# Local attention with biases of full height, paired row loads, two banks for the first values and earlier exponentials, and a reordered last tile of the experts

## The chip, the cores and the metric

The kernel runs on one core of a Trainium2 chip. The metric is the device time of one launch in microseconds (us), the median of several runs. The engines are named as the profile names them: PE is TensorE (PEld its weight loads), ACT is ScalarE, DVE is VectorE, POOL is GpSimd, SP is SyncE, which here only issues DMAs. Each engine works through its own list in order; semaphores tie the lists together.

## What is computed

The input is 8 sequences of 512 rows of 256 values. Four layers follow one another, each added to the rows it gets: causal attention, a feed-forward layer with attention and four experts, a local attention, and the same feed-forward layer again.

```python
x = x + attn_a(layernorm(x), ...)
x = x + ffn(layernorm(x), ...)       # attention, then the expert that a router picks for each row
x = x + attn_b(layernorm(x), ...)    # the local attention
x = x + ffn(layernorm(x), ...)
```

The change touches the third layer and the end of both expert stages. In the third layer the roles of the axes are swapped: at each of the 512 positions the 8 sequences attend to one another, with 16 heads of 16 values and a table of relative keys.

```python
qkv = einsum('tbe,fe->tbf', query, in_proj_weight) + in_proj_bias
scores = einsum('btd,bsd->bts', q, k) + einsum('btd,tsd->bts', q, rel_k)
attn = einsum('bts,bsd->btd', softmax(scores), v)
out = attn @ out_w.T + out_b
```

The experts compute `relu(x @ W1[e] + b1[e]) @ W2[e] + b2[e]` for the expert `e` of each row, and a second layernorm.

## The kernel before

**Stages.** The program runs the causal attention and the first feed-forward attention interleaved, then the first expert stage (`experts`, k = 0), then `local_attention`, then the second feed-forward attention, and the second expert stage (k = 1). Between stages there is a barrier of all engines.

**Local attention.** The positions are cut into four blocks `bt` of 128 (one per partition). A block holds 8 tiles `t`, one for each sequence, of 128 x 256 values. The steps of a block are:

- ACT normalises the tiles (`norm`, L2299) with a mean and a deviation that DVE (`stats`, L2398, L2402, and `shift_of`, L2407) and POOL (`inv_std`, L2550, L2552, a power of -0.5) have made. For block 0 this goes in two groups of four tiles, `x_half` and `x_loaded`, each with its own DMA; the other three blocks form one group of 24 tiles (`x_rest`).
- PE transposes the tiles (`transpose_x`, L2167) four at a time, and ACT copies the result out (`read_xT`, L2307).
- PE projects each tile: `project_qk` (a bias matmul, L2177, then two float32 matmuls, L2179, into one of the two banks `a_ps`), and `project_v` (L2190, the bias matmul L2191, and L2193 for the relative keys, into the single bank `b_ps`). ACT reads the banks (`read_qk`, L2321 and L2319, and `read_v`, L2326). A float32 matmul appears as two records in the trace.
- POOL makes six of the eight products of queries and keys (`scores`, L2570) and DVE two; DVE sums all eight (L2434) and, once the first four tiles have their sums and all eight values have been read, forms the maximum and subtracts it (`shift`, L2445 to L2449).
- ACT takes the exponentials of half a block (`exp`, L2338 and L2342), POOL multiplies five tiles of values by them (`values`, L2579, L2583) and DVE three, PE sums over keys (L2222), and DVE divides (`normalise`, L2488).
- PE transposes the result (L2234), multiplies it by the output weights (`project_out`, a bias matmul L2242 before each pair of L2244), and DVE adds the rows (`add_residual`, L2494).

The biases are kept exact as the sum of three bfloat16 rows, `bias3` and `bo3`, which are multiplied by three rows of ones, `ones3`. So every bias matmul contracts over 3 partitions, where all others around it contract over 128.

**What sets the order.** Everything is written out by hand, and the code is the order. While block `bt` passes through POOL and DVE, PE and ACT prepare block `bt + 1`: PE's list for a block is the transposes and the eight projections of the next block, with `transpose_att` and `project_out` of the block before it in between, and then the sums of this block. ACT's list holds the reads of the next block, with `exp(bt, 0)` behind `read_projections(bt + 1, 3)` and `exp(bt, 1)` behind `read_projections(bt + 1, 5)`.

POOL writes its products to a ring of four buffers (`ring`); a buffer is free again when DVE or PE has summed it.

**The experts' end.** An expert stage has 35 tiles (`SLOTS`). For each tile `s` DVE adds bias and row and takes the statistics (`add_x1`, L1823 to L1829), POOL makes the deviation (`inv_std`, L1973, L1977), DVE scales (`finish`, L1835, L1841), and POOL stores the rows with an indirect DMA (`store`, L1982). POOL also gathers the rows to be added (`gather_prev`, L1961) and adds a bias to them (`shift_prev`, L1968). The last lines of POOL's list before are:

```python
    shift_prev(s)              # for s in range(SLOTS)
    if s >= 1:
        inv_std(s - 1)
    if s >= 2:
        store(s - 2)
    if s + 1 < SLOTS:
        gather_prev(s + 1)
...
inv_std(SLOTS - 1)
store(SLOTS - 2)
store(SLOTS - 1)
```

## Time and profile before

| | us |
|---|---|
| median of three runs | 2563.73 |
| the three runs | 2557.81, 2563.81, 2563.73 |
| the profiled execution | 2558.12 |
| its span, first to last instruction | 2556.3 |
| PE busy | 2378.2 (93% of the span) |
| DVE busy | 1843.5 (72%) |
| ACT busy | 1404.6 (55%) |
| POOL busy | 1366.8 (53%) |

The span lies 1.8 us below the time of its own execution, and that execution 5.6 us below the median. The local attention lies between 1418.5 us, where SP issues the load of its first rows, and 1710.9 us, where PE begins the next stage. All positions in the text are us from the start of the span. The shares of busy time are means over the whole span and don't tell which engine holds up a stage; that is read from the timeline of the stage.

### The profile page before, as it was taken

The numbers are of one execution on the slowest core, as the hardware profiler recorded it, in microseconds if no ns is written. First come the engines' busy times: TensorE is split into PE (matmuls) and PEld (weight loads), VectorE is DVE, ScalarE is ACT, GpSimd is POOL, SyncE is SP. The second block draws the span as 40 slices with busy tenths as digits, with TensorE's granted clock in tenths as the row PEclk, the third lists the DMA queues.
The fourth block names the chain that finished last, engine by engine and source line by source line (L and its number), as shares of the span: only waits on it lengthen the run. The fifth ranks groups of instructions, "written<-read, shape, count | busy, mean of one in ns | idle before, by whom it ended". The sixth has DMA issues, their size and how long they took to land. (4 is left out here: it accounts for less than half of the span.)

```text
span 2556.3 us, 45358 instructions
## 1 busy us (share of the span) xinstructions
PE 2378.2 (93%) x14436; PEld 1387.8 (54%) x14436; DVE 1843.5 (72%) x3687; ACT 1404.6 (55%) x2991; POOL 1366.8 (53%) x1416
## 2 busy tenths in 40 slices
PE   5999999999999999989999699978999999989998
PEld 3555555554443444349898366653344444349997
DVE  5999999999778888845333567867778888844333
ACT  3666666665777777753333232214777777653332
POOL 6466666653335555444655579843335555445655
PEclk9999999999999999999999799988999999999999
DMA  5333333433334444334654200015434444244654
GB/s 156 108 110 103 113 103 102 121 108 93 118 110 135 128 136 125 90 120 163 214 197 160 71 1 17 17 63 136 118 110 133 131 133 124 79 137 164 205 193 140
DMA packets 253390, 305.85 MB, mean 120 GB/s; under 512 B 32642, under 2 KB 228321, under 8 KB 253156
## 3 DMA queue, kind: packets, MB, share of 16 engines
q1 hardware_dynamic: 241620, 275.37, 35.8%
q0 software_dynamic: 10176, 26.27, 3.1%
q8 instruction: 120, 1.97, 0.3%
q10 hardware_dynamic: 1360, 1.31, 0.2%
q14 instruction: 114, 0.93, 0.1%
HBM read 210.32 MB, written 92.84 MB: 119 GB/s over the span
## 5 line engine op out<-in xcount | busy, mean ns | idle before, releaser
L705 ACT ACTIVATE prob_af<-sct_af 128x512 f32<-128x512 f32 (+1 forms) x864 | 483.6, 582 | 257.7 <-PE sct_af L513 251.2
L784 DVE TENSOR_REDUCE neg_max_af<-sc_af 128x1 f32<-128x512 f32 (+3 forms) x864 | 548.8, 663 | 90.7 <-PE sc_af L490 84.9
L784 DVE TENSOR_REDUCE neg_max_f<-sc_f 128x1 f32<-128x512 f32 x512 | 333.7, 685 | 78.2 <-PE sc_f L490 74.0
L705 ACT ACTIVATE prob_f<-sct_f 128x512 f32<-128x512 f32 x512 | 289.8, 598 | 135.5 <-PE sct_f L513 132.9
L513 PE MATMUL sct_af<-stack_q_af,stack_k_af 99*128 99x512 bf16 (+3 forms) x1024 | 321.7, 345 | 4.5 <-ACT prob_af L705 3.1
L490 PE MATMUL sc_af<-stack_k_af,stack_q_af 96*128 96x512 bf16 (+3 forms) x1024 | 321.5, 344 | 4.2 <-DVE neg_max_af L784 4.2
L1636 PE MATMUL y_ps_e<-w_r,hT_e 128*128 x1120 | 256.3, 382 | 8.8 <-issue 5.2
L541 PE MATMUL out_af<-prob_af,v_aug_af 128*32 128x512 f32 (+3 forms) x2048 | 233.1, 527 | 15.4 <-DVE prob_af L814 14.2
L814 DVE SCALAR_TENSOR_TENSOR prob_af<-prob_af,w_r 128x512 f32<-128x512 f32 (+2 forms) x224 | 229.4, 1032 | 17.4 <-ACT prob_af L705 16.0
L1823 DVE TENSOR_TENSOR y_e<-y_ps_e,b_e 128x256 f32<-128x256 f32 x70 | 29.7, 425 | 290.9 <-PE y_ps_e L1636 281.2
L1636 PEld LDWEIGHTS y_ps_e<-w_r,hT_e 128*128 128x128 f32 x1120 | 207.2, 190 | 40.6 <-issue 14.9
L1649 PEld LDWEIGHTS hT_ps_e<-xT_e,w_r 128*128 128x128 f32 x1856 | 217.2, 193 | 5.5 <-issue 1.5
L1649 PE MATMUL hT_ps_e<-xT_e,w_r 128*128 128x128 f32 x1856 | 218.9, 277 | 1.3 <-ACT xT_e L1708 1.1
L490 PE MATMUL sc_f<-stack_k_f,stack_q_f 96*128 96x512 bf16 x512 | 196.1, 388 | 13.9 <-DVE neg_max_f L784 7.6
L513 PEld LDWEIGHTS sct_af<-stack_q_af,stack_k_af 99*128 99x128 bf16 x1024 | 97.8, 98 | 198.3 <-ACT prob_af L705 114.4
L1708 ACT ACTIVATE xT_e<-xT_ps_e 128x256 f32<-128x256 f32 x70 | 26.9, 384 | 323.7 <-PE xT_ps_e L1627 312.3
L513 PE MATMUL sct_f<-stack_q_f,stack_k_f 99*128 99x512 bf16 x512 | 195.8, 385 | 5.2 <-ACT prob_f L705 4.0
L1719 ACT ACTIVATE hT_e<-hT_ps_e,b_r 128x128 f32<-128x128 f32 x560 | 152.8, 383 | 32.0 <-issue 24.8
L1077 POOL TENSOR_TENSOR parts_af<-qkf_af,parts_af 128x512 bf16<-128x512 f32 x62 | 80.9, 1304 | 132.6 <-ACT parts_af L683 132.4
L490 PEld LDWEIGHTS sc_af<-stack_k_af,stack_q_af 96*128 96x128 bf16 x1024 | 99.3, 100 | 75.7 <-issue 19.6
L541 PE MATMUL out_f<-prob_f,v_aug_f 128*32 128x512 f32 x1024 | 137.0, 607 | 1.0 <-ACT prob_f L705 0.7
L513 PEld LDWEIGHTS sct_f<-stack_q_f,stack_k_f 99*128 99x128 bf16 x512 | 49.7, 98 | 159.4 <-ACT prob_f L705 118.2
(385 smaller groups left out, 4623.0 us busy)
## 6 DMA issues: line engine op xcount, KB each, us to landing
w_r<-in_f_W_dram SPq DMA_DIRECT2D x66, 1024.0 KB, 5.6
...
```

What stands on the lines that cost most here:

```text
L490: last = nc.tensor.matmul(bank[:, o:o + cols], M.stack_q[0:96, g, h, qt * P:qt * P + P], M.stack_k[0:96, g, h, 0:cols], start=not masked, ...
L513: last = nc.tensor.matmul(bank[:, o:o + T - q0], M.stack_k[0:99, g, h, kt * P:kt * P + P], M.stack_q[0:99, g, h, q0:T], start=not masked, ...
L541: last = nc.tensor.matmul(bank[32 * i:32 * i + 32, q0:T], M.v_aug[:, kt, 4 * g + i, :], M.prob[:, kt % 2, i, 0:T - q0], start=(kt == 0), s ...
L705: nc.scalar.activation(dst, src.rearrange("p (h q) -> p h q", h=len(heads)), ACT.Exp).then_inc(S.exp_done, 1)
L784: nc.vector.tensor_reduce(M.neg_max[:, qt, heads[0]:heads[-1] + 1], src, AX.X, ALU.max, negate=True).then_inc(S.max_done, 1)
L814: nc.vector.scalar_tensor_tensor(out=p, in0=p, scalar=1.0, in1=M.floor[:, g % 2, hs, kt * P:T], op0=ALU.min, op1=ALU.max).then_inc(S.clip_ ...
L1077: nc.gpsimd.tensor_tensor(M.parts[:, j, 1, :], full, top, ALU.subtract).then_inc(S.split_step, 1)
L1636: last = nc.tensor.matmul(y_ps[:, 0:D], hT[s % 2][:, c, :], w2[:, c, e, :], start=(c == 0), stop=(c == FC - 1))
L1649: last = nc.tensor.matmul(hT_ps[2 * (s % 2) + f][:, q * P:q * P + P], w1[n % NW][:, c, cols], xT[:, c, :], start=(c == 0), stop=(c == DC - 1))
L1708: nc.scalar.activation(xT[:, :, :], xT_ps[:, 0:D].rearrange("p (c t) -> p c t", c=DC), ACT.Copy).then_inc(xT_ready, 1)
L1719: last = nc.scalar.activation(hT[s % 2][:, 4 * f + q, :], hT_ps[2 * (s % 2) + f][:, q * P:q * P + P], ACT.Relu, bias=b1[:, e, 4 * f + q:4 ...
L1823: nc.vector.tensor_tensor(y[i][:, :], y_ps[:, 0:D], b2[:, e, :], ALU.add).then_inc(y_ready, 1)
```

## The change

**Biases of full height.** `bias3`, `bo3` and `ones3` get 128 partitions in place of 3. POOL fills the new rows of the biases with zeros during tile 9 of the first expert stage (two more memsets, and the one of `ones3` is taller). The three rows of the biases are loaded as before. The number of matmuls and their columns stay.

**Rows in pairs.** The first four tiles of block 0 are loaded by two DMAs of two tiles (`x_first`, `x_half`), and go through `stats`, `inv_std`, `shift_of`, the normalisation and PE's transposes in two pairs. There is one more group of statistics on DVE and on POOL. PE projects queries and keys of tiles 0 to 3 before it transposes tiles 4 to 7.

**First values from two banks.** In block 0 the values of odd tiles go to `att_ps`, those of even tiles to `b_ps`, so that PE waits for the read of the bank two tiles back. ACT normalises block 1 in pairs of tiles between these reads, no longer before them.

**Exponentials sooner.** `exp(0, 0)` stands behind `read_projections(1, 1)`, and `exp(bt, 0)` of blocks 1 and 2 stands ahead of `read_projections(bt + 1, 3)`.

**Last tile of the experts.** POOL takes `inv_std` of tile 33 ahead of the gather of tile 34, stores tile 32 before the deviation of tile 34, and adds the bias to the gathered rows of tile 34 behind that deviation. DVE finishes tile 33 ahead of `add_x1(34)`.

```diff
             for s in range(SLOTS):
+                if s == SLOTS - 1:
+                    finish(s - 1)
                 add_x1(s)
...
-                if s >= 1:
+                if 1 <= s < SLOTS - 1:
                     finish(s - 1)
...
-            for s in range(SLOTS):
+            for s in range(SLOTS - 1):
                 shift_prev(s)
                 if s >= 1:
                     inv_std(s - 1)
                 if s >= 2:
                     store(s - 2)
-                if s + 1 < SLOTS:
-                    gather_prev(s + 1)
+                if s == SLOTS - 2:
+                    inv_std(s)
+                gather_prev(s + 1)
...
+                    pool.memset(L.bias3[:, :], 0.0)
+                    pool.memset(L.bo3[:, :], 0.0)
...
+            store(SLOTS - 3)
             inv_std(SLOTS - 1)
+            shift_prev(SLOTS - 1)
             store(SLOTS - 2)
             store(SLOTS - 1)
...
-    L.bias3, L.bo3, L.ones3 = sb("bias3", [3, NB_COLS], BF16), sb("bo3", [3, D], BF16), sb("ones3", [3, P], BF16)
+    L.bias3, L.bo3, L.ones3 = sb("bias3", [P, NB_COLS], BF16), sb("bo3", [P, D], BF16), sb("ones3", [P, P], BF16)
...
+    def v_bank(bt, t):
+
+        return att_ps if bt == 0 and t % 2 == 1 else b_ps
...
-            sp.dma_start(x[0][:, 0:4, :], x_in[0][:, 0:4, :]).then_inc(x_half, 16)
+            sp.dma_start(x[0][:, 0:2, :], x_in[0][:, 0:2, :]).then_inc(x_first, 16)
+            sp.dma_start(x[0][:, 2:4, :], x_in[0][:, 2:4, :]).then_inc(x_half, 16)
...
+            def transpose_first():
+
+                for u in range(2):
+                    pe.wait_ge(xn_ready, u + 1)
+                    for c in range(DC):
+                        for t in (2 * u, 2 * u + 1):
+                            last = nc.tensor.transpose(g_ps[c][:, t * P:t * P + P], xn[:, t, c * P:c * P + P], C.ident[:, :])
+                        if u == 1:
+                            last.then_inc(tr_made, 1)
...
-                if n >= 1:
+                bank = v_bank(bt, t)
+                if bt == 0 and t >= 2:
+                    pe.wait_ge(b_read, n - 1)
+                elif bt >= 1:
                     pe.wait_ge(b_read, n)
...
-            transpose_x(0, 0)
-            transpose_x(0, 1)
+            transpose_first()
             pe.wait_ge(L.params, NPARAM)
             pe.wait_ge(L.rel_ready, 1)
             pe.wait_ge(L.bias_placed, 16 * 6)
-            for t in range(NTM):
+            for t in range(4):
+                project_qk(0, t)
+            transpose_x(0, 1)
+            for t in range(4, NTM):
                 project_qk(0, t)
...
-            norm(0, range(4))
-            norm(0, range(4, NTM))
+            norm_first(1, x_first, range(2))
+            norm_first(2, x_half, range(2, 4))
             read_xT(0, 0)
+            norm_first(3, x_loaded, range(4, NTM))
+            for t in range(4):
+                read_qk(0, t)
             read_xT(0, 1)
-            for t in range(NTM):
+            for t in range(4, NTM):
                 read_qk(0, t)
-            norm(1)
+            may_norm(1)
             for t in range(NTM):
                 read_v(0, t)
+                if t < 4:
+                    last = norm_tiles(1, (2 * t, 2 * t + 1))
+                    if t == 3:
+                        last.then_inc(xn_ready, 1)
...
                     read_projections(bt + 1, 1)
+                    if bt == 0:
+                        exp(bt, 0)
                     read_xT(bt + 1, 1)
                     read_projections(bt + 1, 2)
                     if bt >= 1:
                         read_oT(bt - 1, 1)
+                        exp(bt, 0)
                     read_projections(bt + 1, 3)
-                    exp(bt, 0)
```

The first place is ACT's list in block 0, from the transposes of block 1 (`xnT_l`) to the first exponentials (`weight_l`, with the small `s_ps_l` for DVE's own tile). `qk_l` and `vr_l` are the reads of `read_qk` and `read_v`. Before:

```order
1611 L2307 ACTIVATE xnT_l<-g_ps_l 128x512 x2
1612 L2321 ACTIVATE qk_l<-a_ps_l 128x512
1613 L2326 ACTIVATE vr_l<-b_ps_l 128x384
1614 L2321 ACTIVATE qk_l<-a_ps_l 128x512
1615 L2326 ACTIVATE vr_l<-b_ps_l 128x384
1616 L2307 ACTIVATE xnT_l<-g_ps_l 128x512 x2
1617 L2321 ACTIVATE qk_l<-a_ps_l 128x512
1618 L2326 ACTIVATE vr_l<-b_ps_l 128x384
1619 L2321 ACTIVATE qk_l<-a_ps_l 128x512
1620 L2326 ACTIVATE vr_l<-b_ps_l 128x384
1621 L2338 ACTIVATE weight_l<-s_ps_l 128x512
1622 L2342 ACTIVATE s_ps_l<-s_ps_l 128x128
```

And now:

```order
1624 L2339 ACTIVATE xnT_l<-g_ps_l 128x512 x2
1625 L2353 ACTIVATE qk_l<-a_ps_l 128x512
1626 L2358 ACTIVATE vr_l<-b_ps_l 128x384
1627 L2353 ACTIVATE qk_l<-a_ps_l 128x512
1628 L2358 ACTIVATE vr_l<-b_ps_l 128x384
1629 L2370 ACTIVATE weight_l<-s_ps_l 128x512
1630 L2374 ACTIVATE s_ps_l<-s_ps_l 128x128
1631 L2339 ACTIVATE xnT_l<-g_ps_l 128x512 x2
```

The exponentials have moved ahead of two copies of transposes and four reads of projections.

The second place is the head of the local attention on ACT: `w_next` is where the normalised tiles go. Before:

```order
1605 L2299 ACTIVATE w_next<-x_l,shift_x_l,rstd_l 128x256 x8
1606 L2307 ACTIVATE xnT_l<-g_ps_l 128x512 x4
1607 L2321 ACTIVATE qk_l<-a_ps_l 128x512 x6
1608 L2319 ACTIVATE qk_l<-a_ps_l 128x256 x2
1609 L2299 ACTIVATE w_next<-x_l,shift_x_l,rstd_l 128x256 x8
1610 L2326 ACTIVATE vr_l<-b_ps_l 128x384 x8
```

And now:

```order
1605 L2317 ACTIVATE w_next<-x_l,shift_x_l,rstd_l 128x256 x4
1606 L2339 ACTIVATE xnT_l<-g_ps_l 128x512 x2
1607 L2317 ACTIVATE w_next<-x_l,shift_x_l,rstd_l 128x256 x4
1608 L2353 ACTIVATE qk_l<-a_ps_l 128x512 x4
1609 L2339 ACTIVATE xnT_l<-g_ps_l 128x512 x2
1610 L2353 ACTIVATE qk_l<-a_ps_l 128x512 x2
1611 L2351 ACTIVATE qk_l<-a_ps_l 128x256 x2
1612 L2358 ACTIVATE vr_l<-b_ps_l 128x384
1613 L2317 ACTIVATE w_next<-x_l,shift_x_l,rstd_l 128x256 x2
1614 L2358 ACTIVATE vr_l<-att_ps_l 128x384
1615 L2317 ACTIVATE w_next<-x_l,shift_x_l,rstd_l 128x256 x2
```

The second four tiles are normalised behind the first copies, and block 1 is normalised by twos between reads that alternate between two banks.

The third place is POOL's list at the end of the first expert stage: `var_e` and `rstd_e` are `inv_std`, L1961 (now L1963) is the gather, L1968 (now L1970) the addition of the bias, L1982 (now L1984) a store. Before:

```order
776 L1961 DMA x_prev_e<-layer_d,xt_r 128x256
777 L1968 TENSOR_TENSOR x_prev_e<-x_prev_e,be_e 128x256
778 L1973 TENSOR_SCALAR var_e<-mv_e 128x1
779 L1977 TENSOR_TENSOR rstd_e<-var_e,minus_half 128x1
780 L1982 DMA layer_d<-out_e,xt_r 4096x256
781 L1973 TENSOR_SCALAR var_e<-mv_e 128x1
782 L1977 TENSOR_TENSOR rstd_e<-var_e,minus_half 128x1
783 L1982 DMA layer_d<-out_e,xt_r 4096x256 x2
```

And now:

```order
778 L1975 TENSOR_SCALAR var_e<-mv_e 128x1
779 L1979 TENSOR_TENSOR rstd_e<-var_e,minus_half 128x1
780 L1963 DMA x_prev_e<-layer_d,xt_r 128x256
781 L1984 DMA layer_d<-out_e,xt_r 4096x256
782 L1975 TENSOR_SCALAR var_e<-mv_e 128x1
783 L1979 TENSOR_TENSOR rstd_e<-var_e,minus_half 128x1
784 L1970 TENSOR_TENSOR x_prev_e<-x_prev_e,be_e 128x256
785 L1984 DMA layer_d<-out_e,xt_r 4096x256 x2
```

The deviation of tile 33 has moved ahead of the last gather, and the addition to the gathered rows behind the deviation of tile 34.

## Rows read from the trace of the kernel before

**Rows 1.** Windows: start:end, length, busy PE, PEld, DVE, ACT, POOL (instructions), PE clock, DMA.

```profile
1428.00:1440.00 12.00, 11.43 (x29) 5.66 (x30) 7.23 (x23) 5.17 (x10) 0.00 (x0) 0.64 0.37 117
1525.20:1586.20 61.00, 60.66 (x258) 40.31 (x257) 48.11 (x33) 18.16 (x36) 56.74 (x16) 1.00 0.05 18
1586.20:1647.10 60.90, 60.56 (x258) 40.22 (x256) 48.47 (x34) 14.23 (x28) 52.36 (x15) 1.00 0.05 18
```

**Rows 2.** Timeline, experts' end: start, duration, engine, line, operation [idle before, releaser].

```profile
1408.89 0.42 DVE L1823 TENSOR_TENSOR y_e<-y_ps_e,b_e 128x256 f32<-128x256 f32 x1 [2.04 <-PE y_ps_e L1636]
1409.93 0.71 POOL L1968 TENSOR_TENSOR x_prev_e<-x_prev_e,be_e 128x256 f32<-128x256 f32 x1 [1.18 <-DMA x_prev_e<-layer_d,xt_r]
1410.62 0.23 POOL L1973 TENSOR_SCALAR var_e<-mv_e 128x1 f32<-128x1 f32 x1
...
1411.70 1.31 POOL L1982 DMA_INDIRECT layer_d<-out_e,xt_r  x1 [0.20 <-issue]
...
1415.84 0.98 POOL L1982 DMA_INDIRECT layer_d<-out_e,xt_r  x1 [0.42 <-issue]
1418.51 0.38 SPq L2136 DMA_DIRECT2D x_l<-layer_d  x1
```

**Rows 3.** Timeline, head of the local attention, all engines.

```profile
1422.18 1.40 DVE L2398 BATCH_NORM_STATS2 st_l<-x_l 128x6 f32<-128x256 f32 x4 [7.12 <-DMA x_l<-layer_d]
...
1425.78 4.04 ACT L2299 ACTIVATE w_next<-x_l,shift_x_l,rstd_l 128x256 f32<-128x256 f32 x8 [23.75 <-DVE shift_x_l L2407]
...
1427.91 1.97 PE L2167 MATMUL g_ps_l<-ident,w_next 128*128 128x128 f32 x8 [19.17 <-ACT w_next L2299]
...
1432.32 0.60 PE L2177 MATMUL a_ps_l<-bias_l,ones_l 3*128 3x512 bf16 x1
...
1442.89 4.19 POOL L2552 TENSOR_TENSOR rstd_l<-var_l,half_l 128x24 f32<-128x24 f32 x1
```

**Rows 4.** Timeline of PE: the projection of one tile, bias to bias.

```profile
1493.59 0.39 PE L2177 MATMUL a_ps_l<-bias_l,ones_l 3*128 3x512 bf16 x1
...
1495.72 1.03 PE L2190 MATMUL b_ps_l<-w_l,xnT_l 128*128 128x256 f32 x4
...
1496.68 0.22 PE L2191 MATMUL b_ps_l<-bias_l,ones_l 3*128 3x128 bf16 x1
...
1497.48 0.39 PE L2177 MATMUL a_ps_l<-bias_l,ones_l 3*128 3x512 bf16 x1
```

**Rows 5.** Timeline of PE in the first stage: tall bfloat16 matmuls around a float32 group.

```profile
307.42 0.38 PE L524 MATMUL sct_af<-stack_q_af,w_r 99*128 99x512 bf16 x1
307.64 1.03 PE L442 MATMUL gen_af<-wa_o,attT_af 128*128 128x256 f32 x4
308.50 0.38 PE L509 MATMUL sct_af<-mask_kq,ident_bf 128*128 128x512 bf16 x1
```

**Rows 6.** Timeline of block 0, from POOL's scores to PE's sums.

```profile
1452.75 26.94 POOL L2570 TENSOR_TENSOR ring_l<-qk_l 128x2048 f32<-128x2048 f32 x6 [5.66 <-ACT qk_l L2319]
...
1475.56 0.49 ACT L2326 ACTIVATE vr_l<-b_ps_l 128x384 f32<-128x384 f32 x1 [2.02 <-PE b_ps_l L2193]
...
1477.62 0.70 DVE L2449 TENSOR_TENSOR s_ps_l<-s_ps_l,peak_l 128x512 f32<-128x512 f32 x1
...
1494.08 0.59 ACT L2338 ACTIVATE weight_l<-s_ps_l 128x512 f32<-128x512 f32 x1
...
1494.84 3.69 POOL L2579 TENSOR_TENSOR ring_l<-vr_l,weight_l 128x2048 f32<-128x2048 f32 x1 [15.15 <-ACT weight_l L2338]
...
1509.06 3.62 PE L2222 MATMUL att_ps_l<-ring_l,ident 128*128 128x256 f32 x16
```

**Rows 7.** Timeline of block 3: POOL's values, two bias matmuls of the last project_out.

```profile
1665.75 18.26 POOL L2579 TENSOR_TENSOR ring_l<-vr_l,weight_l 128x2048 f32<-128x2048 f32 x5 [0.96 <-ACT weight_l L2338]
...
1702.31 0.28 PE L2242 MATMUL g_ps_l<-bo_l,ones_l 3*128 3x256 bf16 x1 [0.69 <-ACT attT_l L2349]
...
1703.58 0.28 PE L2242 MATMUL g_ps_l<-bo_l,ones_l 3*128 3x256 bf16 x1
```

58 lines of the change are left out of this document (32 added, 26 removed).

## The prediction

> **What bounds the kernel now.** The page gives PE 93% of the span, but that is a mean; the change lies in the local attention and at the ends of the expert stages, so I read those. First the windows of PE there: from the end of block 0's sums (1525.2) to that of block 1's is 61.0 us and to that of block 2's 60.9 us more, and in both PE is busy 60.6 of them, at full clock, POOL 52.4 in the second, DVE 48.5 [rows 1]. So blocks 1 and 2 are PE's. Then the timeline of block 0: POOL makes its six score products from 1452.75 to 1479.69 and then sits idle 15.15 us until ACT's exponentials; DVE had the shifted scores ready at 1478.32, ACT took them at 1494.08 [rows 6]. There the order of ACT's list is the bound. Then the head: rows asked for at 1418.51, in at 1422.18, first projection at 1432.32, with PE at half clock (2.4 GHz is 1.00) [rows 2, 3]. Last the experts' end: the deviation of tile 33 (1410.62) stands behind the gather for tile 34 [rows 2].
>
> **The experts' end, twice.** Before, POOL waits for the gather until 1409.93, adds, takes tile 33's deviation at 1410.62, stores three times, the last at 1415.84 [rows 2]. Now the deviation of tile 33 comes before the gather, about 2.7 us earlier, and the last stores follow the deviation of tile 34. DVE can take y of tile 34 only at 1408.89 [rows 2] and needs 1.6 us for its statistics; `finish(33)` now stands before it and may hold it 0.3 us for a store to land. From 1410.8: deviation 0.9, addition 0.7, two stores of 1.3 and 1.0 with 0.6 between: the last starts at 1414.4 in place of 1415.84, **1.5 us** less (bounds 0, if the landing holds DVE longer, and 2.7, the whole advance). The second expert stage has the same rows, so again 1.5 at the end of the program. The two memsets fall in tile 9; POOL waits for gathers in such tiles (1.18 us even at the last [rows 2]), so 0; uncovered, less than 2 us, since a POOL product of 2048 columns takes 3.65 [rows 7] and they have 1264.
>
> **The head.** The load starts at 1417.0. Two tiles in place of four: before, 3.67 us from issue to DVE's start [rows 2, 3]; I take 3.0 (bounds 2.2 and 3.67). Statistics of two tiles 0.9, POOL's deviation at most 1.3, shift 0.2, two tiles on ACT 1.0: the first pair is normalised at about 1423.4, the second at 1424.5, since each step of the second waits for the same step of the first. Four transposes (1.97 for eight at half clock [rows 3]) and two copies later, at 1426.5, PE projects, against 1432.32 [rows 3]. The new order has a bubble of its own: transposes of tiles 4 to 7 and both copies stand between projection 3 and 4 with nothing beside them, 2.0 us. The clock: a mean of 0.64 over 1428 to 1440 [rows 1] means half speed to about 1436.6, 8.7 us after PE began. PE begins 4.3 us earlier, so I let the clock rise by 1432.3: two projections of 3.84 at half clock (half of the second at full), the others 1.93, the bubble, and the last read: 1447.4. A floor is POOL's deviation of 24 tiles, over at 1447.08 before [rows 3] and at 1445.6 now. POOL's scores start at **1447.4** against 1452.75, 5.3 sooner (bounds 1446.0 and 1449.3, the latter with the next projection slow too).
>
> **Biases of full height.** Sixteen float32 records of 256 columns last 3.62 together, 0.38 alone [rows 6], so one takes (3.62 - 0.38) / 15 = 0.216, one of 512 columns 0.432, one of 128 0.108. A projection takes 3.89 from bias to bias, of which 4 x (0.432 + 0.216 + 0.108) = 3.02 is float32 work [rows 4]; the two short biases cost the other 0.87. In the first stage a bfloat16 matmul of 99 or 128 partitions and 512 columns costs 0.22 before a float32 group, and the group (0.86 for 4 x 0.216) loses nothing to the one behind it [rows 5]. By these rows the biases should cost 0.22 and 0.06: a projection 3.30, **0.59 less**. A bias of 256 columns goes from 1.27 - 0.86 = 0.41 [rows 7] to 0.11, 0.30 less. Bounds: 0 and these values; I take these, since the rows are of the same engine, types and widths.
>
> The Trainium skill (TensorEngine Tiling (Array Packing), Key Properties) says that a change of the tiling mode drains the engine; a contraction over 3 rows could be such a mode, and that would be the 0.3 us.
>
> **Block 0.** Eight values are read with two normalised tiles between the first four reads: 1.53 us each on ACT, later 1.3 on PE, so the last is read at about 1459.3 against 1476.05 [rows 6]. DVE's shift waits now for POOL's fourth product (1447.4 + 18.05) and ends at 1469.9. Then ACT, which has reached the exponentials at 1468.0, takes them at once: done at 1470.6. POOL is not through with its scores before 1474.4, so the **15.15 us wait goes whole**, and what is late next is POOL itself. Its values take 18.2 + 7.3 = 25.5: over at 1499.9 in place of 1520.38. PE sums tiles 0 and 1 from 1488.0, waits 1.2 for the third product (1492.6) and ends at 1504.8 against 1525.2: **20.4 us**, which is 5.3 + 15.15. ACT held at the exponentials for 1.9 us delays two copies, which PE first needs for projection 4, 3.3 us after; no cost.
>
> **Blocks 1 and 2.** PE's cycle holds eight projections and eight output biases: 8 x 0.59 + 8 x 0.30 = 7.1 less, 53.8 us. POOL's is 52.4 and DVE's work 48.5 [rows 1], so both now press. Walking the lists, POOL never waits long; DVE's first `normalise` comes 2.0 us late behind its own products, which delays nothing in the next projections but carries into block 3. I take 0.5 us for small waits: cycles of 54.3, **6.6 us less each**, 13.2. In block 3 DVE's chain sets POOL's start, 2.1 us later by the carried delay. So POOL's last values start 20.4 + 13.2 - 2.1 = 31.5 us sooner, at 1634.2 in place of 1665.75 [rows 7]. `exp(1, 0)` and `exp(2, 0)` follow DVE's shift within 0.3 us in this walk, ahead of POOL's need.
>
> **The tail.** After the last sums, eight output biases lie in a row on the path: 8 x 0.30 = **2.4 us**.
>
> **The sum.** 31.5 (with the first 1.5 of the experts) + 2.4 + 1.5 = **35.4 us** from the profiled execution's 2558.12: 2522.7. The median of before lies 5.6 above that execution, two of three runs being near 2563.8 and one at 2557.8. Carried over, 2528.3; I give 2528.
>
> **Rivals.**
>
> *The cycles don't follow PE.* With PE at 53.8, POOL at 52.4 and DVE waiting on both, the lists may interlock: PE's sums need POOL's last product, DVE's own products come behind `normalise`, PE's next projections need those. For it: only 1.4 us of room, and a DVE list that is near 50 before any wait. Against it: DVE had 12.5 us of idle time per cycle [rows 1]. At 57.5 us a cycle 6.4 us are lost: 2528.3 + 6.4 = 2535.
>
> *A bias costs the same at any height.* Then only order counts. The head loses 2.5 us (eight projections), block 0's sums become PE's (eight projections of 3.89 from about 1463) and end at 1511.5, 13.7 sooner; the cycles and the tail stay; 15.2 with the end of the program: 2548.5. For it: the tall matmuls of the first stage stand next to other work than these. Against it: nothing is lost there at a change of type or width, so the height is what is left [rows 5].
>
> The Trainium skill (TensorE: Matmul & The Clock Gate, Why this matters for your kernels) says that one matmul of a short contraction takes the same time as one of 128 rows. By that the change of height gives nothing, and the time would be the one of this rival; the trace speaks against it as far as rows 4 and 5 can be compared.
>
> *The clock falls.* PE, quicker now, waits for POOL and DVE, and after waits it runs at half speed. The row for it: after 19.17 us of idle time PE needed 8.7 us to get back, in which it lost 4.3 us [rows 1, 3]. One such spell per block costs 4 x 4.3 = 17 us and gives 2545; from eight or nine spells on, two per block, the gain of 35.4 is used up, and at ten the program is slower, 2571. It decides if PE's waits in the cycles grow to several us; I count 1.2 us in block 0 and less after, where before they are 0.3 us of 61.
>
> **How the numbers follow.** Forecast 0.66, with a range of 2518 to 2536: from all of it and runs at the lower level (2522.7 - 4) to a bias that saves half of what rows 5 say on PE's cycles, head and tail (+7.5). Interlocked cycles 0.19 (2535, to 2541). Same cost at any height 0.09 (2548). The clock 0.06: half of that near one spell or two per block, 2545 to 2563, half beyond. The 80% range takes in the forecast and the interlocked cycles, and a start of the scores at its late bound: 2517 to 2541. A measurement of this kernel can tell some 0.3% (7.7 us) from no change. Faster by more than that: 0.66 + 0.19 + 0.09 = 0.94; within it 0.03; slower 0.03.
>
> **What would show each step.** Right, if bias matmuls of 512 columns are followed after 0.22 us and a projection takes 3.3 us; if POOL's first values start without a wait near 1474; if the windows between ends of sums are near 54 us with PE still busy over 95%; if the last store of the first expert stage starts near 1414.4 and the first projection near 1426.5. Wrong, if PE's cycle shows new idle time ahead of the sums (POOL) or of the projections (DVE's own products), if the clock column falls below 1.00 within blocks 0 to 2, or if the distance behind a bias stays at 0.3.

## The result, and the profile of the changed kernel

The changed kernel takes 2521.38 us (median of 4 executions, 2520.16 to 2521.58) beside 2563.77 of the kernel before (4 executions, 2557.81 to 2564.4): a ratio of 0.984, 95% interval 0.982 to 0.986. A second set of the changed kernel on another chip gave 2526.72 beside 2565.46, ratio 0.985 [0.983, 0.987]. The forecast was 2528, with a range of 2517 to 2541. The two profiled executions lie 36.7 us apart (2558.12 and 2521.44; spans 2556.3 and 2519.7); the sum of the prediction was 35.4.

In the tables below *local stage* is the distance from the issue of the local attention's first row load (SPq, `x_l<-layer_d`) to the first matmul of the next stage (`gen_f<-ident` at L416). It was 292.36 us before (1418.51 to 1710.87) and is 260.77 now (1417.50 to 1678.27), 31.6 less. The load itself is issued 1.0 sooner, and the rest of the program, with the second expert stage at its end, is 4.0 shorter (845.4 and 841.4; it varies by some us between executions, see below). 1.0 + 31.6 + 4.0 = 36.6.

First the windows of PE, as [rows 1]: start:end, length, busy time of PE, PEld, DVE, ACT, POOL (instructions), granted clock, DMA. The last two run from the end of one block's sums to the end of the next one's, as the last two of [rows 1] do.

```profile
1428.00:1440.00 12.00, 11.21 (x34) 5.36 (x33) 7.22 (x23) 4.67 (x10) 0.00 (x0) 0.94 0.30 97
1507.50:1561.70 54.20, 53.86 (x258) 40.65 (x257) 46.93 (x33) 18.13 (x36) 53.01 (x15) 1.00 0.06 20
1561.70:1615.90 54.20, 53.86 (x258) 40.66 (x257) 48.21 (x34) 14.18 (x28) 52.33 (x15) 1.00 0.06 20
```

The same 258 instructions of PE now take 54.2 us in place of 61.0 and 60.9, at the same full clock, and PE still has under 0.4 us idle in each. POOL and DVE do the same work as before. POOL is busy for 53.0 and 52.3 us of the 54.2. So the cycle is still PE's.

The timeline of the experts' end, as [rows 2]: start, duration, engine, line, operation [idle before, releaser]. Lines left out are marked by three dots.

```profile
1407.65 0.25 POOL L1975 TENSOR_SCALAR var_e<-mv_e 128x1 f32<-128x1 f32 x1
...
1410.02 0.42 DVE L1823 TENSOR_TENSOR y_e<-y_ps_e,b_e 128x256 f32<-128x256 f32 x1 [0.36 <-issue]
...
1411.67 0.23 POOL L1975 TENSOR_SCALAR var_e<-mv_e 128x1 f32<-128x1 f32 x1 [0.28 <-DVE mv_e L1829]
...
1414.83 0.98 POOL L1984 DMA_INDIRECT layer_d<-out_e,xt_r  x1 [0.31 <-issue]
1417.50 0.38 SPq L2147 DMA_DIRECT2D x_l<-layer_d  x1
```

Tile 33's deviation starts 3.0 us sooner than in [rows 2], DVE reaches tile 34 1.1 us later (PE's matmuls for it were 0.6 later in this execution, the rest is `finish(33)`, which stands ahead of it now), and the last store starts at 1414.83 (forecast 1414.4).

The timeline of the head and of the first block, all engines, as [rows 3, 6]:

```profile
1426.68 0.59 PE L2199 MATMUL a_ps_l<-bias_l,ones_l 128*128 128x512 bf16 x1 [0.84 <-ACT xnT_l L2339]
...
1429.94 0.38 PE L2199 MATMUL a_ps_l<-bias_l,ones_l 128*128 128x512 bf16 x1
...
1447.07 26.99 POOL L2614 TENSOR_TENSOR ring_l<-qk_l 128x2048 f32<-128x2048 f32 x6
1447.14 4.47 DVE L2448 SCALAR_TENSOR_TENSOR shift_x_l<-mv_l,rstd_l 128x24 f32<-128x24 f32 x1 [4.69 <-POOL rstd_l L2596]
...
1452.19 1.13 PE L2215 MATMUL b_ps_l<-w_l,xnT_l 128*128 128x256 f32 x4 [3.88 <-ACT vr_l L2358]
...
1470.67 0.70 DVE L2490 TENSOR_TENSOR s_ps_l<-s_ps_l,peak_l 128x512 f32<-128x512 f32 x1
...
1471.56 0.59 ACT L2370 ACTIVATE weight_l<-s_ps_l 128x512 f32<-128x512 f32 x1
...
1491.95 3.62 PE L2247 MATMUL att_ps_l<-ring_l,ident 128*128 128x256 f32 x16
```

ACT takes the exponentials 0.9 us after DVE starts its shift (16.5 in [rows 6]). POOL's first value product follows at 1474.01 with no wait, where it stood idle 15.15 us. But the head shows something that the prediction does not have: **DVE's shift of 24 tiles (the instruction that makes `shift_x_l`) lasts 4.47 us**, and ends with POOL's first product, which takes 4.5 us here. ACT needs that shift before it normalises block 1, ahead of the first value read. So PE waits 3.88 us for a value bank, and behind that its clock falls to the lower level of 1.2 GHz for a while. Two windows of 4 us:

```profile
1452.00:1456.00 4.00, 3.81 (x15) 3.07 (x15) 4.00 (x3) 3.83 (x9) 4.00 (x1) 0.66 0.00 0
1456.00:1460.00 4.00, 4.00 (x26) 3.58 (x25) 4.00 (x3) 2.08 (x5) 4.00 (x2) 0.91 0.00 0
```

The clock is at the lower level once more in block 3, behind a wait of 4.13 us for DVE's addition at 1625.84. In the kernel before, PE waited 1.65 us in that place and the clock stayed at 1.00. A window of 8 us:

```profile
1624.00:1632.00 8.00, 5.47 (x18) 4.29 (x19) 8.00 (x6) 1.19 (x2) 8.00 (x3) 0.50 0.00 0
```

This spell held nothing up: ACT takes the exponentials of block 3 at 1635.10, 0.03 us behind DVE's shift, and POOL starts its values behind them. At the start of block 3's sums the clock is low in both kernels (0.50 from 1640 to 1644 now, 0.50 and 0.56 from 1668 to 1676 before).

Last, the timeline of block 3 and the tail, as [rows 7]:

```profile
1635.87 18.25 POOL L2623 TENSOR_TENSOR ring_l<-vr_l,weight_l 128x2048 f32<-128x2048 f32 x5 [1.64 <-ACT weight_l L2370]
...
1664.57 0.28 PE L2267 MATMUL g_ps_l<-bo_l,ones_l 128*128 128x256 bf16 x1 [0.74 <-ACT attT_l L2381]
...
1665.56 0.27 PE L2267 MATMUL g_ps_l<-bo_l,ones_l 128*128 128x256 bf16 x1
```

The output biases follow each other after 0.98 us on average (four in a row, 1664.57 to 1667.51), not 1.27.

### The profile page after: what moved, and what is told of

The parts are those of the page before. It is cut to its first block and busy times, and to the rows that moved or that the text cites. A ratio compares the mean times of both kernels' runs of the same rounds, so it can differ in the third digit from the quotient of the medians.

```text
span 2519.7 us, 45366 instructions
## 1 busy us (share of the span) xinstructions
PE 2351.4 (93%) x14436; PEld 1392.6 (55%) x14436; DVE 1857.4 (74%) x3688; ACT 1402.0 (56%) x2991; POOL 1360.1 (54%) x1420
## 5 line engine op out<-in xcount | busy, mean ns | idle before, releaser
L705 ACT ACTIVATE prob_af<-sct_af 128x512 f32<-128x512 f32 (+1 forms) x864 | 483.0, 582 | 257.9 <-PE sct_af L513 252.6
L814 DVE SCALAR_TENSOR_TENSOR prob_af<-prob_af,w_r 128x512 f32<-128x512 f32 (+2 forms) x224 | 237.6, 1071 | 14.1 <-ACT prob_af L705 12.9
L1719 ACT ACTIVATE hT_e<-hT_ps_e,b_r 128x128 f32<-128x128 f32 x560 | 152.3, 382 | 31.6 <-issue 24.3
```

The lines of the kernel that those rows point to most:

```text
L705: nc.scalar.activation(dst, src.rearrange("p (h q) -> p h q", h=len(heads)), ACT.Exp).then_inc(S.exp_done, 1)
L814: nc.vector.scalar_tensor_tensor(out=p, in0=p, scalar=1.0, in1=M.floor[:, g % 2, hs, kt * P:T], op0=ALU.min, op1=ALU.max).then_inc(S.clip_ ...
L1719: last = nc.scalar.activation(hT[s % 2][:, 4 * f + q, :], hT_ps[2 * (s % 2) + f][:, q * P:q * P + P], ACT.Relu, bias=b1[:, e, 4 * f + q:4 ...
```

## The experiments

Eleven runs. All but `bias_only` start from the changed kernel. Each has one part undone, a size changed or a wait added; two repeat a kernel. "Ratio" is against the kernel before on the same chip; where it is missing, one execution was taken.

| kernel | edit | time, us | ratio [95%] | local stage, us |
|---|---|---|---|---|
| before | | 2563.77 | 1 | 292.36 |
| changed | | 2521.38 | 0.984 [0.982, 0.986] | 260.77 |
| `short_bias` | biases over 3 partitions again | 2539.28 | 0.993 [0.990, 0.996] | 278.70 |
| `bias_only` | before, with tall biases alone | 2542.46 | 0.992 [0.989, 0.994] | 273.23 |
| `heights` | biases over 64, 96 and 32 partitions | 2537.54 | | 271.17 |
| `late_exp` | first exponentials late again | 2523.98 | 0.986 [0.983, 0.990] | 266.3 |
| `one_bank` | one value bank, block 1 normalised in one piece | 2537.04 | 0.991 [0.988, 0.995] | 275.01 |
| `norm_whole` | two banks, block 1 in one piece | 2526.22 | | 264.72 |
| `pool_waits` | POOL waits for the last shift | 2520.14 | 0.986 [0.983, 0.989] | 257.88 |
| `again_waits` | the same kernel again | 2520.82 | 0.984 [0.982, 0.985] | 258.32 |
| `again` | the changed kernel again | 2526.72 | 0.985 [0.983, 0.987] | 260.84 |
| `four_rows` | rows loaded and transposed by four | 2521.83 | 0.984 [0.981, 0.988] | 258.19 |
| `old_experts` | old order of the experts' last tile | 2528.21 | 0.986 [0.982, 0.990] | 258.26 |

The total moves by several us from one execution to the next of one kernel (2511.8 to 2524.9 for `again_waits`), in stages that no edit touches: in the profiles the row load is issued anywhere from 1409.3 to 1421.8, and what follows the local stage takes 840.7 to 849.8. The local stage does not: two profiles of one kernel differ by 0.07 (260.77, 260.84) and 0.44 (257.88, 258.32). So parts worth a few us are judged by the stage and not by the total.

### The biases

`short_bias` (without the two new memsets as well):

```
-    L.bias3, L.bo3, L.ones3 = sb("bias3", [P, NB_COLS], BF16), sb("bo3", [P, D], BF16), sb("ones3", [P, P], BF16)
+    L.bias3, L.bo3, L.ones3 = sb("bias3", [3, NB_COLS], BF16), sb("bo3", [3, D], BF16), sb("ones3", [3, P], BF16)
```

> The changed kernel with the biases back at 3 partitions, all else as changed. If the height of the bias matmuls is what PE's cycle gained (my theory): a projection takes 3.89 us again in place of 3.35, the cycles of blocks 1 and 2 are 61 us in place of 54.2, block 0 loses about 4 us, the tail 2: about 2541 us, 20 above the changed kernel. If the height costs nothing and PE's cycle shrank through the order of the lists: 2521 to 2523, and projections stay at 3.35.

Measured: the local stage is 17.9 us longer, each block takes 60.9 us again (transposes of the next block at 1506.22, 1567.11 and 1627.99), a projection 3.89. Timeline of PE, one projection of `short_bias`, and the same of the changed kernel, from bias to bias:

```profile
1482.99 0.39 PE L2197 MATMUL a_ps_l<-bias_l,ones_l 3*128 3x512 bf16 x1
1483.30 1.98 PE L2199 MATMUL a_ps_l<-w_l,xnT_l 128*128 128x512 f32 x4
1485.12 1.03 PE L2213 MATMUL b_ps_l<-w_l,xnT_l 128*128 128x256 f32 x4
1486.08 0.22 PE L2214 MATMUL b_ps_l<-bias_l,ones_l 3*128 3x128 bf16 x1
1486.24 0.71 PE L2216 MATMUL b_ps_l<-w_rel_l,xnT_l 128*128 128x128 f32 x4
1486.88 0.39 PE L2197 MATMUL a_ps_l<-bias_l,ones_l 3*128 3x512 bf16 x1
```

```profile
1478.55 0.38 PE L2199 MATMUL a_ps_l<-bias_l,ones_l 128*128 128x512 bf16 x1
1478.76 1.88 PE L2201 MATMUL a_ps_l<-w_l,xnT_l 128*128 128x512 f32 x4
1480.48 1.03 PE L2215 MATMUL b_ps_l<-w_l,xnT_l 128*128 128x256 f32 x4
1481.34 0.22 PE L2216 MATMUL b_ps_l<-bias_l,ones_l 128*128 128x128 bf16 x1
1481.40 0.66 PE L2218 MATMUL b_ps_l<-w_rel_l,xnT_l 128*128 128x128 f32 x4
1481.90 0.38 PE L2199 MATMUL a_ps_l<-bias_l,ones_l 128*128 128x512 bf16 x1
```

Here the distances between starts are what counts, not the durations, which hardly differ. Around a short bias three of them grow by some 0.1 us each: from the group ahead of it to the bias (0.96 and 0.86 ahead of the bias of 128 columns), from the bias to its group (0.31 and 0.21; 0.16 and 0.06), and from that group to the next (1.82 and 1.72). A short bias costs its neighbours too, 0.27 us for each of the two of a projection.

The 17.9 us are a net figure. With short biases POOL's scores start later, DVE's shift gets in ahead of them and takes 0.18 us again (at 1442.30), so `short_bias` does not pay what the changed kernel pays in its head. Against `pool_waits`, which doesn't pay it either, short biases cost 20.8 us. The same holds for `heights` below (shift 0.18, 13.3 us over `pool_waits`).

`bias_only` is the other side of it:

```
 pool.memset(L.ones3[:, :], 1.0)
+pool.memset(L.bias3[:, :], 0.0)
+pool.memset(L.bo3[:, :], 0.0)
```

with the three tensors [P, ...] as in the change.

> The kernel before, with biases of full height and nothing else changed. Theory: the cheaper bias gives 0.54 us per projection and 0.3 per output bias wherever PE sets the pace: blocks 1 and 2 fall from 61.0 to about 54.5 us each, the head gains 2 to 3 us (six or eight projections at half or full clock) and the tail 2.4; POOL's wait for the late exponentials of block 0 stays, though shorter, since ACT reaches them behind projections that are quicker: 13 in place of 15.15. Local stage 292.4 - 13 - 4 - 2.4 = 273, total about 19 us less than before, 2539 where before has 2558. Rival: with the late exponentials the blocks interlock (POOL late, PE waits, clock falls) and the biases alone bring less than 12 us.

Measured: 19.1 us off the local stage (273.23, expected 273), blocks of 54.2 us, POOL's wait for the exponentials 12.55. The total is 0.8% less. So the tall biases alone bring half of what the change brings in the total and 19.1 of the 31.6 us in the local stage, and they need none of the other edits. The cycles don't interlock; in block 0 PE waits 2.66 us for POOL, and its clock falls for a few us.

`heights` asks what it is about 3 partitions:

```
-nc.tensor.matmul(a_ps[t % 2][:, :], ones3[:, :], bias3[:, 0:2 * D], start=True, stop=False)
+nc.tensor.matmul(a_ps[t % 2][:, :], ones3[0:64, :], bias3[0:64, 0:2 * D], start=True, stop=False)
-nc.tensor.matmul(bank[:, D:D + P], ones3[:, :], bias3[:, 3 * D + r0:3 * D + r0 + P], start=True, stop=False)
+nc.tensor.matmul(bank[:, D:D + P], ones3[0:96, :], bias3[0:96, 3 * D + r0:3 * D + r0 + P], start=True, stop=False)
-nc.tensor.matmul(ys, ones3[:, :], bo3[:, :], start=True, stop=False)
+nc.tensor.matmul(ys, ones3[0:32, :], bo3[0:32, :], start=True, stop=False)
```

> The changed kernel, with its bias matmuls cut to other heights: 64 partitions for the bias of 512 columns, 96 for that of 128 columns, 32 for the output bias of 256 (the rows left out are zeros). What is measured is the distance behind each: at full height 512 columns cost 0.22 us before the float32 group, the projection of one tile 3.35 us, two output biases and their groups 0.98 us from bias to bias of one tile; over 3 partitions a projection took 3.89. Theory: a short bias is dear because the height of the contraction changes between neighbours, so any height that the engine handles as a lower one costs the same as 3 partitions, some 0.27 us more: 64 and 32 are dear, 96 is cheap (the first stage had 99 partitions at no cost). Then a projection takes 3.35 + 0.27 = 3.62, an output bias 0.3 more, and the total is 4 to 12 us over the changed kernel's 2521. Rival: only heights that are no multiple of 32 are dear; then all distances and the total stay as in the changed kernel.

Its timeline of PE, a projection and two output biases in block 1:

```profile
1527.43 0.39 PE L2199 MATMUL a_ps_l<-bias_l,ones_l 64*128 64x512 bf16 x1
1527.74 1.98 PE L2201 MATMUL a_ps_l<-w_l,xnT_l 128*128 128x512 f32 x4
1529.57 1.03 PE L2215 MATMUL b_ps_l<-w_l,xnT_l 128*128 128x256 f32 x4
1530.43 0.22 PE L2216 MATMUL b_ps_l<-bias_l,ones_l 96*128 96x128 bf16 x1
1530.49 0.66 PE L2218 MATMUL b_ps_l<-w_rel_l,xnT_l 128*128 128x128 f32 x4
1531.08 0.28 PE L2267 MATMUL g_ps_l<-bo_l,ones_l 32*128 32x256 bf16 x1
1531.29 1.13 PE L2269 MATMUL g_ps_l<-w_o_l,attT_l 128*128 128x256 f32 x4
1532.35 0.28 PE L2267 MATMUL g_ps_l<-bo_l,ones_l 32*128 32x256 bf16 x1
```

64 partitions cost what 3 do (0.31 to the group, and 1.83 for it), 32 as well (1.27 from output bias to output bias, as in [rows 7]), 96 nothing (0.06, and 0.86 ahead of it). The theory holds: the price is not that of a height below 128 as such, nor of one that is no multiple of 32. 64 and less pay it between neighbours of 128, 96 does not. Blocks took 59.0 us (1507.26, 1566.23, 1625.20), 4.8 more than the changed kernel's: 8 x 0.3 for the 64 rows and 8 x 0.3 for the 32. The local stage is 10.4 us longer. The 4 to 12 us expected were for the total, and the total of this one execution is 16.2 over the changed kernel's, outside of them; 5.4 of these lie behind the local stage (846.8 us in place of 841.4), where no edit is.

The Trainium skill (TensorEngine Tiling (Array Packing), Key Properties) says that a change of the tiling mode drains the engine, and (Tiling Modes) lists modes of 32, 64 and 128 rows. The trace agrees: 3, 32 and 64 rows cost alike, 96 and 99 nothing. That the array's mode is the cause is still read from this pattern, no row names it.

### The first exponentials

`late_exp` puts `exp(0, 0)` back behind projection 3:

```
                     read_projections(bt + 1, 1)
-                    if bt == 0:
-                        exp(bt, 0)
                     read_xT(bt + 1, 1)
                     read_projections(bt + 1, 2)
                     if bt >= 1:
                         read_oT(bt - 1, 1)
-                        exp(bt, 0)
                     read_projections(bt + 1, 3)
+                    exp(bt, 0)
```

> The changed kernel with exp(bt, 0) back behind read_projections(bt + 1, 3). My theory: with the quicker PE, ACT reaches the exponentials of block 0 some 5.5 us later than now, POOL waits that long, but PE's sums are only 2.4 us later, and in blocks 1 and 2 nothing is lost because PE sets the cycle: 2524, 2 to 3 above the changed kernel. Rival, that the 15 us wait of POOL comes back in full and counts: 2536.

Measured: the total is 2523.98, as expected, but it is no finer than some us. The local stage is 5.5 us longer, twice the expected 2 to 3. POOL waits 6.96 for the weights, and PE for POOL (timeline, then two windows of 2 us):

```profile
1480.05 3.68 POOL L2621 TENSOR_TENSOR ring_l<-vr_l,weight_l 128x2048 f32<-128x2048 f32 x1 [6.96 <-ACT weight_l L2370]
...
1498.38 3.44 PE L2247 MATMUL b_ps_l<-ring_l,ident 128*128 128x256 f32 x8 [2.65 <-POOL ring_l L2625]
```

```profile
1498.00:1500.00 2.00, 1.62 (x4) 1.35 (x5) 1.97 (x2) 0.00 (x0) 2.00 (x2) 0.50 0.00 0
1500.00:1502.00 2.00, 2.00 (x8) 1.65 (x7) 2.00 (x1) 0.00 (x0) 2.00 (x2) 0.67 0.00 0
```

POOL's wait was foreseen; PE's clock was not: the windows show half clock behind PE's wait of 2.65, so the eight matmuls took 3.44 us, where the changed kernel's took 1.89. Not all of the 5.5 us belong to the edit. Up to the start of the sums, `late_exp` is already 1.1 us behind the changed kernel (75.56 us after the load is issued in place of 74.45), and all of that arises ahead of the place that the edit touches: behind a wait of 3.21 us PE's first matmuls run at half clock at once (2.07 us for the group at 1451.23, 1.13 in the changed kernel). From the start of the sums to their end it takes 19.90 us in place of 15.55. In the kernel with all the rest of the change, then, the earlier exponentials are worth **4.4 us**, not the 15.15 of the wait that they remove: with the late order POOL waits 6.96 here, and PE is busy with projections for most of it. That they bring as much or as little when added alone to the kernel before was not run.

### The value banks and the pieces of block 1

`one_bank` undoes both:

```
-        return att_ps if bt == 0 and t % 2 == 1 else b_ps
+        return b_ps
...
-            may_norm(1)
+            norm(1)
             for t in range(NTM):
                 read_v(0, t)
-                if t < 4:
-                    last = norm_tiles(1, (2 * t, 2 * t + 1))
-                    if t == 3:
-                        last.then_inc(xn_ready, 1)
```

> The changed kernel with the first values through one bank and block 1 normalised in one piece before the reads, as in the kernel before. My theory: block 1's projections start about 7 us later (1471 in place of 1464), and since PE is the bound from there to the end of the sums, all of it is lost: 2528 to 2529. Rival, that POOL's list hides it: under 2523.

Measured: the local stage is 14.2 us longer, twice what I expected. PE waits 8.80 us at the first value (DVE's blocked shift, then 4.04 for eight tiles) and then runs at half clock, with a read every 3.72 us (10 us windows of PE):

```profile
1450.00:1460.00 10.00, 6.73 (x19) 5.05 (x20) 10.00 (x5) 3.04 (x7) 10.00 (x3) 0.50 0.00 0
1460.00:1470.00 10.00, 8.26 (x30) 6.14 (x30) 5.18 (x3) 1.47 (x3) 9.98 (x3) 0.65 0.00 0
```

`norm_whole` keeps the two banks and undoes the pieces alone.

> The changed kernel with both value banks, but ACT normalises the eight tiles of block 1 in one piece ahead of the first value. With one bank and one piece the local stage was 275.0 us, 14.2 longer than the changed kernel's, PE waiting 8.80 us at the first value and the reads coming every 3.72 us at half clock. Theory: the piece before the reads costs the wait of about 8.5 us and the clock that falls with it, the second bank lets PE work during a read (a read every 1.5 to 2.6 us in place of 2.3 to 3.7): block 1's transposes come 4 to 8 us later than in the changed kernel, not 14: local stage 265 to 269. Rival 1: the single bank was all of it, and the stage is 258 to 262. Rival 2: the piece was all of it, and it is 272 to 276.

Measured: 264.72, 3.9 us more than the changed kernel, just under the expected 265. PE waited 7.48 us, and came back to full clock within 5 us. So the pieces are worth 4 us with two banks, and taking the second bank away as well costs 10 more: with one bank PE pauses 0.58 us at each read, and stays at half clock until about 1467, 15 us behind the wait. One bank with the pieces kept was not run, so how the 10 us split when the wait is short is open.

### DVE's shift and POOL's first product

`pool_waits` has one line more than the changed kernel:

```
+            pool.wait_ge(shift_done, 4)
             for bt in range(NBT):
                 for t in POOL_QK:
                     scores(bt, t)
```

> The changed kernel; POOL waits for DVE's shift of the last 24 tiles (shift_done 4) before its first product. In the changed kernel that DVE instruction, which took 0.18 us before, lasts 4.47 us and ends with POOL's first product, and ACT and PE wait for it. My theory: the two block each other, so with the wait it takes 0.2 us, POOL starts 0.2 later, ACT reads the first values 4.3 us sooner, PE starts block 1 some 3.5 us sooner, and the sums of block 0 end 2.5 us sooner, where POOL becomes the limit: 2519. Rival, that the instruction is slow for another reason: it stays at 4.4 us and the time at 2521.5 or 0.2 above.

Timeline of `pool_waits` in the same place:

```profile
1445.93 0.18 DVE L2448 SCALAR_TENSOR_TENSOR shift_x_l<-mv_l,rstd_l 128x24 f32<-128x24 f32 x1 [4.69 <-POOL rstd_l L2596]
...
1447.38 4.49 DVE L2460 TENSOR_TENSOR own_l<-qk_l,a_ps_l 128x2048 f32<-128x2048 f32 x2 [1.26 <-ACT qk_l L2351]
1447.49 18.04 POOL L2614 TENSOR_TENSOR ring_l<-qk_l 128x2048 f32<-128x2048 f32 x4 [1.59 <-ACT qk_l L2351]
```

The shift takes 0.18 us, PE waits for no value bank, its clock stays full there, and the local stage is 2.9 us shorter although POOL starts no sooner (30.2 us after the load is issued, 29.6 in the changed kernel). The DVE products beside POOL's (L2460, one input from SBUF and one from PSUM) last 2.2 us each and are not held: the shift, with both inputs in SBUF, is. The changed kernel has a second such pair, at the end of the first expert stage. DVE's first step of `finish(34)` (L1835, both inputs in SBUF) starts at 1412.58, 0.04 us behind the `shift_prev(34)` on POOL that the change put there, and takes 0.95 us where it took 0.48 before. The last store doesn't wait for it.

The Trainium skill (SBUF — State Buffer, Who interferes with whom) says that a DVE instruction with two SBUF inputs contends with a GpSimd instruction that reads SBUF, since its second input comes through a read interface that the two share, and that the order of issue decides who blocks. The trace agrees: POOL's product started at 1447.07 and the shift at 1447.14, and it took 4.47 us, ending with the product; it took 0.18 where POOL stood still. Below this is called the lock.

Was the fall of the clock behind it chance? `again` and `again_waits` are the two kernels a second time.

> The changed kernel itself, a second time. In its first profile POOL's first product held DVE's shift for 4.47 us, PE waited 3.88 us for a value bank and then ran some 3 us of work at half clock; the kernel with the old end of the experts has the same head, waited 3.00 us there and stayed at full clock, and its local stage was 258.3 us long in place of 260.8. Theory: the lock (4.4 to 4.5 us in DVE's shift) is there in every execution, while the fall of the clock behind PE's wait comes or stays away with the start of the stage, so the local stage is 258 or 261 us, the blocks keep their 54.2 us, and the experts' last store comes 9.17 us after the last group of their matmuls, as in the first profile. Rival: old_experts differs in something else that matters, and the changed kernel always has the fall: 260.8 again. Total 2518 to 2524.

> The changed kernel with POOL waiting for the last shift before its first product, a second time, beside the changed kernel on the same chip. Theory: the shift lasts 0.2 us, PE doesn't wait for a value bank, the clock stays full, and the local stage is 257.9 us again whatever its start; against the changed kernel that is 0.4 us where that one keeps its clock and 2.9 where it loses it, so the totals differ by 0 to 3 us, less than the spread of single executions. Rival: the 257.9 of the first look was luck of the clock too, and it spreads as the changed kernel does.

`again`: the shift takes 4.48, PE waits 3.62, the clock falls, 260.84. `again_waits`: no wait and 258.32. The difference of 2.5 to 2.9 us in the local stage is there in both pairs of profiles. The totals do not show it by their intervals (0.985 [0.983, 0.987] and 0.984 [0.982, 0.985]). `old_experts`, whose local attention is that of the changed kernel, had the blocked shift and a wait of 3.00 us and kept its clock (timeline of PE, then the window of 4 us behind the wait):

```profile
1455.96 1.13 PE L2210 MATMUL b_ps_l<-w_l,xnT_l 128*128 128x256 f32 x4 [3.00 <-ACT vr_l L2353]
```

```profile
1455.00:1459.00 4.00, 3.04 (x19) 2.65 (x20) 4.00 (x3) 3.58 (x8) 4.00 (x2) 1.00 0.00 0
```

Its local stage is 258.26. From that first matmul to the transposes of block 1 it took 8.6 us, the changed kernel 10.3: the half clock costs 1.7 and the longer wait 0.9, together the 2.5 us. So the fall of the clock is no necessary part of the lock: the same code of the local attention ran with it and without. But that rests on one profile. Both profiles of the changed kernel itself have the fall and 260.8 us, which is what the rival expected; how often it stays away is open. The lock itself was there in all of them.

`four_rows` loads, normalises and transposes the first rows by four tiles, as before the change:

```
-            sp.dma_start(x[0][:, 0:2, :], x_in[0][:, 0:2, :]).then_inc(x_first, 16)
-            sp.dma_start(x[0][:, 2:4, :], x_in[0][:, 2:4, :]).then_inc(x_half, 16)
+            sp.dma_start(x[0][:, 0:4, :], x_in[0][:, 0:4, :]).then_inc(x_half, 16)
...
-            transpose_first()
+            transpose_x(0, 0)
+            transpose_x(0, 1)
...
-            for t in range(4):
-                project_qk(0, t)
-            transpose_x(0, 1)
-            for t in range(4, NTM):
+            for t in range(NTM):
                 project_qk(0, t)
```

(and the steps of ACT, DVE and POOL to match).

> The changed kernel with the first rows loaded, normalised and transposed by four tiles again, as before the change, and all six projections behind them. My theory: loading in pairs starts the projections about 4 us sooner (first one 9.1 us after the load is issued in place of about 13.8) and costs a bubble of 2 us between projections 3 and 4; taken back, POOL's scores start about 3 us later and block 0's sums about 4 later, and the local stage is 3 to 5 us longer than the changed kernel's 260.8: a total of 2524 to 2526. Rival: since POOL's scores start at once behind its deviation of 24 tiles, which also has to wait for the rows, and DVE's shift then stands beside POOL's product, the order of loading moves nothing, or the shift gets in before POOL and the later start is even quicker: local stage 257 to 261.

The rival was right: 258.19, 2.6 us *less* than with pairs. Its first projection starts 13.9 us after the load is issued, with pairs 9.2, but POOL's first product 30.7 after it against 29.6. Timeline of `four_rows`:

```profile
1441.14 0.18 DVE L2442 SCALAR_TENSOR_TENSOR shift_x_l<-mv_l,rstd_l 128x24 f32<-128x24 f32 x1 [4.68 <-POOL rstd_l L2587]
...
1443.16 9.06 POOL L2605 TENSOR_TENSOR ring_l<-qk_l 128x2048 f32<-128x2048 f32 x2 [2.05 <-ACT qk_l L2348]
```

Of 4.7 us at the first projection 1.2 are left at POOL. 1.8 go into the bubble between projections 3 and 4 (1435.74 to 1437.57 in the changed kernel), 0.6 into a first projection that runs longer at half clock, and 1.1 into POOL's deviation of 24 tiles, which does not come sooner with the projections: it ends 29.6 us after the load is issued with pairs and 28.7 with fours. And what is won makes POOL ready for its product in the instant in which DVE wants its shift. Pairs with POOL's wait (257.9 and 258.3) and fours without it (258.2) come out alike. **The loading in pairs brings nothing** in this kernel.

### The experts' last tile

`old_experts` restores the order in both expert stages:

```
-            for s in range(SLOTS - 1):
+            for s in range(SLOTS):
                 shift_prev(s)
...
-                if s == SLOTS - 2:
-                    inv_std(s)
-                gather_prev(s + 1)
+                if s + 1 < SLOTS:
+                    gather_prev(s + 1)
...
-            store(SLOTS - 3)
             inv_std(SLOTS - 1)
-            shift_prev(SLOTS - 1)
```

> The changed kernel with the last tile of the experts in the old order, in both expert stages. Theory: the new order brings 1.0 us at the end of the first stage and 1.5 at the end of the program, so the load of the local stage's rows is issued 1.0 later, at 1418.5 in place of 1417.5, the local stage stays at 260.8, and the total is 2521.4 + 2.5 = 2524. Rival: the stores wait for something else at the end of the program, and only the 1.0 of the first stage or nothing is lost: 2521.5 to 2522.5.

The times of the stores themselves shift from execution to execution, so I measure from the last group of expert matmuls (PE, `y_ps_e`, x16). Its start in the four profiles stands at 1405.03 (before), 1405.66 (changed), 1408.33 (`old_experts`), 1405.13 (`again`); the last store follows 10.81, 9.17, 10.82 and 9.19 us later. The new order is worth **1.6 us** in the first stage; I had read 1.0 from the two profiles, as PE happened to be 0.63 later in the changed one. (Over all profiles with the new order the distance is 8.86 to 9.68, so 1.1 to 2.0 us.) At the end of the program the distance is 11.20 before and 10.84 in `old_experts` and `bias_only`, and 8.81 to 9.91 in the ten profiles with the new order: 0.9 to 2.4 us. The ratio (0.986 [0.982, 0.990]) can't tell it from the changed kernel. The total of 2528.21 is 4 over the 2524 expected, with the load issued at 1421.81 and not at 1418.5, since PE's last group itself came 2.7 us later in this execution.

## Why the prediction was right, step by step

**The bound.** That blocks 1 and 2 are PE's, and stay so, is what carried it: 54.2 us each against 54.3 forecast. The small waits that I allowed for did not come: PE had 0.34 us idle. The projection took 3.35 and not 3.30, which used up the rest. The output bias was right (0.98, so 0.29 less; 0.30 forecast).

**The rivals.** *Interlock* (57.5 us a cycle) fell: with 1.2 and 1.9 us between PE's cycle and POOL's work each still finds its work ready. *Same cost at any height* fell by the rows of `short_bias` and `heights`. What the Trainium skill (TensorE: Matmul & The Clock Gate, Why this matters for your kernels) says of a short contraction is not contradicted in the time of the matmul itself (0.39 and 0.38); what the matmul does to its neighbours is not in that sentence. *The clock falls* happened twice, and in small. In block 0's head 3.88 us of wait and about 1.7 lost at half clock delayed the sums; in block 3 the spell that the kernel before did not have cost nothing. The cycles of blocks 1 and 2 stayed at 1.00.

**Block 0.** The sums ended at 1507.50, not 1504.8, so block 0 gained 17.7 us in place of 20.4. This is the step that failed. I forecast the last value read at 1459.3 "with two normalised tiles between the first four reads"; it ended at 1463.17. The walk had the shift of block 1's rows at 0.2 us, from [rows 3], where POOL stood still beside it. In the changed kernel POOL's first product starts in that instant. So the projections of block 1 began at 1464.26 in place of about 1460.7, and the sums at 1491.95 in place of 1488.0. They were now PE's, not POOL's: the end was 2.7 late, since the 1.2 us wait for POOL's third product was gone. With the lock removed (`pool_waits`) the sums start 1487.83 and wait 1.37 for POOL, as forecast. POOL's own times were right (scores 1447.07 for 1447.4, values 1474.01 for 1474.4), and its 15.15 us wait went whole.

**What these steps are worth.** The forecast added 5.3 (head) and 15.15 (wait) to 20.4 in block 0. The parts undone one by one give another picture: tall biases 17.9, banks and pieces 14.2, exponentials 5.5 (4.4 without the difference in the head), pairs -2.6, out of 31.6 in the local stage. They sum to 35.0 (33.9), more than the whole: undo one, and part of what the others won comes back as a wait (POOL waits 12.92 us for the exponentials in `one_bank`, 6.96 in `late_exp`), and the lock and the clock in the head differ from one of these kernels to the next. Of the biases both sides were run, 17.9 undone and 19.1 by themselves. My sum was close for all edits together; the 15.15 read as the price of the exponentials would have been over three times too large.

**Head.** First projection 1426.68 (1426.5). The clock rose before 1429.94 and not at 1432.3: the projection that starts there is followed after 1.93 us by the next (1431.87), the full-clock distance. So the last read ended at 1445.89, ahead of the forecast 1447.4. But the floor was higher: POOL's deviation of 24 tiles ended at 1447.1, not 1445.6, although the load was issued sooner. The scores waited for the floor and not for the reads. That they started at 1447.07, near the forecast 1447.4, is two errors that cancel: luck.

**Carried delay and tail.** POOL's last values started at 1635.87 (1634.2): 2.7 late from block 0, 0.2 gained in the cycles, and the carried delay of DVE 1.4 in place of 2.1 (20.0 us behind block 2's sums, before 18.6). From there to the next stage 42.40 us in place of 45.12: 2.7 less, forecast 2.4. Of these 2.15 lie behind the last sums, where the output biases are (15.47 us from their end to the next stage, before 17.62), and 0.6 in the sums of block 3, whose first matmuls run at half clock in both kernels, for a shorter time now.

**Experts.** 1.6 for 1.5 in the first stage, and 2.4 for 1.5 at the end of the program between the two profiles.

**The offset.** 2528 was 2522.7 from the sum and 5.6 for the distance of the median from the profiled execution. The median of the changed kernel lies on its profiled execution (2521.38 and 2521.44). The sum was 1.3 off, and part of that is luck too. By the forecast the load came 1.5 us sooner, the local stage was 32.4 shorter and the rest 1.5; measured are 1.0, 31.6 and 4.0. Of the last 4.0, 2.4 are at the last stores; the other 1.6 arose in stages that no edit touches. The 5.6 was not a property of the kernel but of which executions were caught, as the later sets show (2558.17, 2563.67 and 2565.46 for the kernel before). It is the larger part of the distance of 6.6 us between 2528 and 2521.4.
